# Attention, then routed experts, on one core: the causal mask of the transposed scores moves from TensorE to GpSimd, and the query and key products are laid over six steps

## The reference, cut to what matters

```
h = clip(curve(x @ ccm)) @ conv          # 8 pictures of 256 rows x 256, as tokens
h = concatenate([h, txt], axis=1)        # 8 x 384 tokens of 256 features
xn = layernorm(h)
ckv = xn @ W_DKV                         # 64 wide
q, k, v = xn @ W_UQ, ckv @ W_UK, ckv @ W_UV      # 16 heads of 16
scores = where(causal, q @ k.T / 4, -inf)        # per head, 384 x 384
h = h + (softmax(scores) @ v) @ W_O
h = h + moe(layernorm(h))                # 8 experts, top 2, capacity 384, gelu, 256-1024-256
```

## Time and profile before

| what | us |
|---|---|
| median of three runs | 706.63 |
| the profiled execution's own time | 704.81 |
| its span | 703.1 |
| TensorE busy in it | 639.8 (91%) |
| VectorE busy | 400.3 (57%) |
| ScalarE busy | 377.8 (54%) |
| GpSimd busy | 305.5 (43%) |

### The profile page before, as it was taken

The page is one execution under the profiler, slowest core; times in us unless marked ns, Lnnn a source line. Parts: engine busy times, 40 slices in busy tenths (PEclk is TensorE's granted clock), DMA queues, the critical chain, the costliest instruction groups (busy, mean ns, idle before and its releaser), DMA issues.

```text
span 703.1 us, 14382 instructions
## 1 busy us (share of the span) xinstructions
PE 639.8 (91%) x5488; PEld 533.9 (76%) x5488; DVE 400.3 (57%) x1005; ACT 377.8 (54%) x800; POOL 305.5 (43%) x415
## 2 busy tenths in 40 slices
PE   2799899998999999999988699999999999999991
PEld 2556565665666657567667699999999999999990
DVE  4887585687777877757766353444444444444310
ACT  4466766747667576565561265555555554555530
POOL 3300001004121141220426497888888888888222
PEclk9999999999999999999999889999999999999996
DMA  7448391714424043153103443444444444442222
GB/s 260 113 119 230 97 269 52 199 47 134 118 68 131 9 112 93 56 144 129 63 17 103 127 143 76 106 106 106 106 106 106 106 106 106 106 106 47 23 25 28
DMA packets 66477, 73.76 MB, mean 105 GB/s; under 512 B 6312, under 2 KB 61458, under 8 KB 66408
## 3 DMA queue, kind: packets, MB, share of 16 engines
q1 hardware_dynamic: 55584, 59.27, 27.8%
q0 software_dynamic: 9504, 13.00, 10.9%
q10 hardware_dynamic: 1320, 0.57, 0.3%
HBM read 31.62 MB, written 22.35 MB: 77 GB/s over the span
## 4 chain that ended last, share of the span: by engine, by line
PE 67%; DVE 12%; ACT 7%; issue 5%; DMA 3%; SPq 3%; POOL 1%; ACTq 0%; DVEq 0%; POOLq 0%
PE t_bank L1654 19%; PE bank L1669 12%; PE s_bank L1669 6%; PE bank L662 5%; DVE mx L1111 3%; PE t_bank L626 3%; PE t_bank L720 3%; SPq L392 3%; PE s_bank L604 3%; ACT part L978 2%; PE bank L690 2%; PE s_bank L1640 2%; DVE wr L1166 2%; PE t_bank L627 1%; PE s_bank L605 1%
## 5 line engine op out<-in xcount | busy, mean ns | idle before, releaser
L1613 DVE TENSOR_TENSOR hl<-h,hh 128x384 fp32r<-128x384 f32 x128 | 104.5, 818 | 155.7 <-ACT h L1571 155.7
L1111 DVE TENSOR_REDUCE mx<-s_bank 128x2 f32<-128x256 f32 (+2 forms) x192 | 122.6, 683 | 51.9 <-PE s_bank L605 51.3
L1568 ACT ACTIVATE hh<-t_bank 128x384 fp32r<-128x384 f32 x128 | 63.0, 492 | 133.9 <-PE t_bank L1654 131.7
L919 ACT ACTIVATE pt<-t_bank 128x512 f32<-128x512 f32 x128 | 76.8, 601 | 65.8 <-PE t_bank L627 64.8
L1538 POOL DMA_INDIRECT out<-yo,xr x48 | 75.0, 1564 | 72.6 <-ACT yo L1579 62.9
L1526 POOL TENSOR_TENSOR wl<-wr,wh 128x256 fp32r<-128x256 f32 x112 | 94.5, 878 | 1.2
L1654 PE MATMUL t_bank<-xh,wh 128*128 128x384 f32 x256 | 87.2, 341 | 0.0
L1654 PE MATMUL t_bank<-xl,wh 128*128 128x384 f32 x256 | 86.8, 339 | 0.0
L1654 PE MATMUL t_bank<-xh,wl 128*128 128x384 f32 x256 | 86.7, 338 | 0.0
L626 PE MATMUL t_bank<-qs,ks 98*128 98x384 bf16 (+2 forms) x384 | 85.2, 274 | 0.6 <-ACT pt L917 0.4
L604 PE MATMUL s_bank<-ks,qs 96*128 96x128 bf16 (+2 forms) x384 | 78.3, 273 | 5.4 <-DVE mx L1111 4.6
(11 more groups left out here) (191 smaller groups left out, 1433.6 us busy)
## 6 DMA issues: line engine op xcount, KB each, us to landing
wr<-in_w SPq DMA_DIRECT2D x16, 1024.0 KB, 5.7
qs<-part SPq DMA_DIRECT2D x96, 96.0 KB
ks<-part SPq DMA_DIRECT2D x90, 96.0 KB
slot_rows<-empty SPq DMA_DIRECT2D x4, 1560.0 KB, 9.3
xr<-slot_rows SPq DMA_DIRECT2D x16, 390.0 KB, 3.3
wr<-in_x SPq DMA_DIRECT2D x8, 768.0 KB, 5.4
out<-hid SPq DMA_DIRECT2D x8, 384.0 KB
qs<-mT ACTq DMA_DIRECT2D x64, 3.0 KB
```

Source lines behind the costliest of these rows:

```text
L919: ins = act.activation(pt[:, p, unit // 2, 0:AT[1]], bank, ACT.Exp)
L1111: ins = dve.tensor_reduce(mx[:, p // 2, j, 2 * (p % 2):2 * (p % 2) + 2], pair_region(s_bank, j), AX_X, ALU.max)
L1568: act.activation(hh[:, f, :], h_banks[f % NH], ACT.Gelu_apprx_tanh)
L1613: dve.tensor_tensor(hl[:, f, :], h[f % 2][:, :], hh[:, f, :].bitcast(F32), ALU.subtract).then_inc(hl_done, 1)
```

## The change

The mask matmul of line 627 and `mask_k` go. In their place GpSimd sets the part of each diagonal block that the mask hides to zero in `pt`, after the exponential, by an `affine_select` for each unit (`clip`: two blocks of 128 x 128, 192 calls in all), and `values` waits for those (`clipped`) and no longer for the exponentials. GpSimd's program is written anew around the clips: three in each step, with the sends, powers and bias additions between them, one bias addition behind each clip of p = 3.

The twelve stages of `query_key` stand two to a step (`ahead`): in the odd turn stage (0,0) at p = 1, then (0,1), (0,2) at p = 2, then (1,0), (1,1) at p = 3; in the even turn (1,2), (2,0) at p = 0, then (2,1), (2,2) at p = 1, then (3,0), (3,1) at p = 2, and (3,2) at p = 3. `project(b, 0)` goes to `M[1]`, both `token_values` and all `contexts_out` to `M[0]`, and `token_values(b + 1, 0)` moves from p = 1 of the even turn to its p = 0. The sync engine stacks k = 0 and 1 in the odd turn, and k = 2 and 3 in the even one.

```
+    def ahead(n, p, place):
+        b = n // 2 + (2 if n % 2 else 1)
+        i = 2 * p + place + (-3 if n % 2 else 5)
+        return (b, *divmod(i, 3)) if late(b) and 0 <= i < 12 else None
...
     def project_bank(b, k):
-        return s_bank[:, 2, :] if b == B - 1 and k else M[0]
+        if k == 0:
+            return M[1]
+        return s_bank[:, 2, :] if b == B - 1 else M[0]
...
                 elif live(b + 1):
-                    for i in range(3):
-                        stack(sp, b + 1, 3, i)
+                    for k in (2, 3):
+                        for i in range(3):
+                            stack(sp, b + 1, k, i)
...
+        def clip(n, p, unit):
+            pool.wait_ge(exp_done, 3 * (4 * n + p) + unit + 1)
+            if unit == 1:
+                blocks = pt[:, p, :, AT[1]:AT[1] + P]
+            else:
+                blocks = pt[:, p, unit // 2, 0:AT[1]].rearrange("p (i c) -> p i c", c=P)[:, 0:4:3, :]
+            pool.affine_select(out=blocks, in_=blocks, compare_op=ALU.is_ge, fill=0.0, base=0,
+                               pattern=[[0, 2], [1, P]], channel_multiplier=-1).then_inc(clipped, 1)
...
         for n in range(FIRST, LAST):
+            b, odd = n // 2, n % 2
+            for p in range(4):
+                for unit in range(3):
+                    if turn_live(n):
+                        clip(n, p, unit)
+                    if odd and (p, unit) == ((2, 0) if turn_live(n) else (0, 0)) and live(b - 1):
+                        rstds2(b - 1)
+                    if odd and p == 3 and live(b - 1) and b < B:
+                        residual(b - 1, unit)
+                if odd:
+                    if p == 1 and live(b - 2):
...
+                        send(b - 2, 0)
+                    if p == 2 and live(b - 2):
+                        send(b - 2, 1)
...
+                else:
+                    if p < 2 and live(b - 3) and n <= OVER:
+                        send(b - 3, 3 + p)
+                    if p == 2 and live(b + 2):
+                        rstds(b + 2)
+                    if p == 3 and live(b - 3) and n <= OVER:
+                        send(b - 3, 5)
...
     def shifted_scores(n, p, unit):
...
-                pe.matmul(bank[:, col:col + w], k[:, h, j * P:(j + 1) * P], q[:, h, j * P:T], start=True, stop=False)
-                mm = pe.matmul(bank[:, col:col + P], ident_b[:, :], mask_k[:, :], start=False, stop=True)
+                mm = pe.matmul(bank[:, col:col + w], k[:, h, j * P:(j + 1) * P], q[:, h, j * P:T], start=True, stop=True)
...
     def values(n, grp):
-            pe.wait_ge(exp_done, 3 * (4 * n + 2 * grp + 2))
+            pe.wait_ge(clipped, 3 * (4 * n + 2 * grp + 2))
```

More of the change, by code:

```diff
@@ L307, in front @@
     exp_done = sem("exp_done")
+    clipped = sem("clipped")
     pv_done = sem("pv_done")
@@ L456, in sync @@
                 elif live(b + 2):
-                    for k in range(3):
+                    for k in (0, 1):
                         for i in range(3):
@@ L549, in gpsimd @@
         for n in range(FIRST, LAST):
[L550 to L581, removed]
@@ new lines, in gpsimd @@
+            b, odd = n // 2, n % 2
[9 more added lines that the diff above has]
+                    if p == 1 and live(b - 2):
+                        if b == 2:
+                            pool.wait_ge(zeroed, 16 * (PIECES + 1))
+                        pool.wait_ge(slot_done, b - 1)
+                        send(b - 2, 0)
+                    if p == 2 and live(b - 2):
+                        send(b - 2, 1)
+                    if p == 3 and live(b - 2):
+                        if n < OVER:
+                            send(b - 2, 2)
+                        else:
+                            for i in range(2, TOPK * NT):
+                                send(b - 2, i)
+                else:
+                    if p < 2 and live(b - 3) and n <= OVER:
[4 more added lines that the diff above has]
+                        send(b - 3, 5)
@@ L685, in project @@
             pe.wait_ge(cn_sb, 2 * b + 2)
-            take("last" if b == B - 1 and k else 0, hid_add, 2 * b + k + 1)
+            take(1 if k == 0 else "last" if b == B - 1 else 0, hid_add, 2 * b + k + 1)
             dst = project_bank(b, k)
@@ L772, in tensor @@
         pe.wait_ge(consts, 5)
-        pe.wait_ge(masks, 6)
+        pe.wait_ge(masks, 4)
         pe.wait_ge(relu_done, CH)
@@ L816, in tensor @@
                     latents(b + 2, 1)
-                if odd and p >= 2 and late(b + 2):
-                    query_key(b + 2, p - 2, 2)
-                if not odd and p < 2 and late(b + 1):
-                    query_key(b + 1, 2 + p, 2)
+                if ahead(n, p, 0):
+                    query_key(*ahead(n, p, 0))
                 if n == FIRST and p == 3:
@@ L835, in tensor @@
                         query_key(1, k, 1)
-                if odd and late(b + 2):
-                    if p == 0:
-                        tokens_back(b + 2, 0, 1)
-                    else:
-                        query_key(b + 2, p - 1, 0)
-                if not odd and p == 0 and late(b + 1):
-                    query_key(b + 1, 3, 0)
+                if odd and p == 0 and late(b + 2):
+                    tokens_back(b + 2, 0, 1)
+                if ahead(n, p, 1):
+                    query_key(*ahead(n, p, 1))
                 if p == 0 and prev:
@@ L1021, in scalar @@
                 if p == 3 and prev:
-                    contexts_out(n - 1, 0 if odd else 1)
+                    contexts_out(n - 1, 0)
                 if odd and p == 1 and late(b + 2):
                     tokens_back(b + 2, 1, 1)
-                if odd and p >= 2 and late(b + 2):
-                    query_key(b + 2, p - 2, 1)
-                if not odd and p < 2 and late(b + 1):
-                    query_key(b + 1, 2 + p, 1)
                 if cur:
@@ L1055, in scalar @@
                     max_rows(n + 1, 0)
-                if odd and late(b + 2):
-                    if p == 0:
-                        tokens_back(b + 2, 0, 1)
-                    else:
-                        query_key(b + 2, p - 1, 0)
-                if not odd and p == 0 and late(b + 1):
-                    query_key(b + 1, 3, 0)
+                if odd and p == 0 and late(b + 2):
+                    tokens_back(b + 2, 0, 1)
+                if ahead(n, p, 1):
+                    query_key(*ahead(n, p, 1))
+                if not odd and p == 1 and live(b + 1):
+                    token_values(b + 1, 1, 0)
                 if n == 0 and p == 0:
@@ L1079, in scalar @@
                     contexts(n, 0)
+                if not odd and p == 0 and live(b + 1):
+                    token_values(b + 1, 0, 0)
                 if not odd and p == 0 and live(b + 2):
                     relus(b + 2, 0)
-                if not odd and p == 1 and live(b + 1):
-                    token_values(b + 1, 0, 0)
-                    token_values(b + 1, 1, 1)
                 if n == FIRST and p == 0:
```

31 lines of the change are left out of this document (9 added, 22 removed).

## The result

The changed kernel takes 693.01 us (median of four runs, 692.11 to 693.17), the one before 705.79 beside it (703.58 to 707.01): a ratio of 0.9826, with 95% between 0.9804 and 0.9849. The forecast was 686 us. The sign and the range held; the gain is 12.8 us where 21 were forecast. The profiled execution after took 693.07 us, 11.7 less than the 704.81 of before.

The account below looks back on a forecast made before the run. TensorE was taken to bound about 32 of each 44.6 us period, VectorE the other 12.6. Six periods gave 17 us and turns 0, 13, 14, 15 gave 4: 21 off 704.81, plus 1.8 to the median, 686 us; range 675 to 702.

Parts of the forecast that it names:

- The sum of the middle periods: Six two-turn periods with late batches: 3.3 us gained, less 0.3 port and 0.2 second norm, 2.8 each, 17 us in all.
- Spread and bank: Middle period: 0.4 us net from products moved out of TensorE's stretch, 0.8 from copy waits, 0.2 from the bank.
- the bank: Maxima's transpose waited 0.74 us for VectorE's row addition holding its bank; moving `project(b, 0)` was to save 0.2 a period.
- the 32 masks that matter: Of 48 mask matmuls a period, 32 lie where TensorE sets the pace: 0.058 us each, 1.86 us; the rest worth nothing.
- The 0.8 us for copies: TensorE's waits for ScalarE's copies of parts, 1.6 us a period, were to halve with two stages a step.
- Turns 0, 13, 14 and 15 have masks alone, 1.39 each, of which I count 1.0: 4.: Turns outside the six periods gain only from the removed masks, 4 us together.
- The values' matmuls show no wait for them: Sign: TensorE's value products never wait for clips, since 1.7 us separates exponential and values at p = 2, even turn.
- The colour steps: Sign: VectorE's colour steps, two inputs in SBUF, 736 to 794 ns in the turns, rise by at most a tenth.
- The port and the second norm: Losses a middle period: 0.3 us for VectorE's port shared with GpSimd, 0.2 for the norm's power queued behind a clip.
- Rival A: VectorE takes the period, so half the masks and none of the smoothing count: 8 us gained, 698; chance 0.17.
- Rival B: All 1.6 us of copy waits and 0.7 of the bank's go each period: 33 us gained, 673; chance 0.05.
- Rival C: GpSimd becomes late, TensorE waits for clips ahead of values: 14 us slower, 721; decides from 0.8 us clips; chance 0.10.

Follow-up runs that it names:

- experiment 10: The spread of the stages alone, both masks kept, with `project(b, 0)` back in `M[0]`; ratio 0.9923 to the kernel before.
- Experiment 4: The changed kernel with no clip run, diagonal blocks left unmasked and `values` waiting for the exponentials; 685.18 us, ratio 0.9718 to the kernel before.
- experiment 3: The changed kernel with odd-turn bias additions behind all clips of p = 3 on GpSimd and the first send a step later; 690.06 us, ratio 0.9791.
- experiment 1: The kernel before with only the clips in place of the second mask, stages and banks as they were; ratio 1.0006.
- experiment 6: The kernel before with one edit, the output projection of two tiles in the other bank; ratio 0.9940.
- experiment 2: The kernel before with only the spread of stages, new banks and stacking; both masks and the old GpSimd program stay; ratio 0.9844.
- experiment 8: The changed kernel with each clip done twice, the second after the first has ended; ratio 0.9997 to the kernel before.
- experiment 5: The changed kernel with odd-turn sends 0, 1, 2 and then the bias additions behind all clips of p = 3 on GpSimd; ratio 0.9798.

## Why the prediction was right in direction and 7 us off in size

**The sum of the middle periods held, its terms not quite.** 17 us were forecast, turns 1 to 12 gave 16.8; the period fell by 2.93 us, forecast 2.8. That it is so close is luck: two errors of 2 us cancel. Spread and bank brought 10.5 us where 6 x (0.4 + 0.8 + 0.2) = 8.4 were forecast. The term that was too small is the bank: I took 0.2 of a 0.74 us wait, and the wait of 0.80 us a period went entirely. How much of the 10.5 is the bank's is less sure, since experiment 10 has a delay of its own. The clips over the masks brought 6.3 on top where 6 x (1.86 - 0.3 - 0.2) = 8.2 were forecast. The price of the 32 masks that matter was too high, since part of their time came back as waits for copies. The 0.8 us for copies is right for the spread alone (1.48 to 0.72 a period) and wrong for the sum (1.38 with the masks gone): the masks that leave were part of the time in which the copies were made. Two terms that share a cover can't both be counted.

**The step that failed: "Turns 0, 13, 14 and 15 have masks alone, 1.39 each, of which I count 1.0: 4."** They lost 1.1 us. Experiment 4 splits it: without clips turn 0 is 0.3 and turns 13 to 15 are 1.9 us shorter than before, so the masks were worth 2.2 there, not 4. With clips the same parts are 0.8 and 2.4 us longer than without. The 2.4 us stand against a sum that had a price for clips only in six middle periods. The 0.8 us of turn 0 are not the clips' work: experiment 3 has the same clips there and takes 16.9 us against 16.8, and the profiled execution after has the 3.4 us at the lower clock. One execution of each kernel was profiled; such a fall in turn 0 stands in six of the ten kernels without the second mask (17.6 to 18.9 us; 16.2 to 17.0 in the other four) and in none of the four with it. That the emptier list lets it happen is likely, and not shown.

**What the sum did not have: the end of the turns.** Behind the last exponential 3.4 us were lost. "The values' matmuls show no wait for them" is right in the middle, where rows 4 and 7 had 1.7 us of cover, and wrong at the end: there the last value product is on the path, nothing runs beside it, and its clip stands behind a send and two bias additions. The wait for the clip (1.15 us) and the slow values (2.79 us for 1.50) are in the rows above. How much of the 3.4 us they are is less clear. 1.5 us come back in experiment 3 and 1.7 in experiment 4, without a clip; but experiment 1, with the wait and with values at full clock, takes 41.9 us, and so does experiment 6, without a clip. The other 1.7 or so is in experiments 2, 3 and 4 alike (40.4 to 40.6 against 38.7), with a granted clock of 0.71 in 370 to 380 us of experiment 2. The profiled execution of before stands at 0.50 for 8.0 us of this stretch, that of after for 14.8, and every other kernel profiled for 9.5 or more, with or without masks and clips. So a part of the 3.4 us can be that one execution's good fortune: four of the kernel before differ by 3.4 us (703.58 to 707.01). The prediction read no row of this stretch. The cause of the second half, and of the 1.0 us ahead of the first exponential (45.5 to 47.0 in all runs), stays open.

**Checked by the sum**: 21 forecast, less 0.2 (turns 1 to 12), 5.1 (bare turns), 3.4 (end), 1.0 (start), plus 0.3 (rest) is 11.6; measured 11.7. The profiled execution of before lies 1.0 us below the median of its four runs, that of after at its median, where I had allowed 1.8; so the profiled time missed 683.8 by 9.3 us, and the median missed 686 by 7.0.

**Smaller points.** A clip was forecast at 0.42 us; the median is 0.406. The colour steps' mean rose from 0.747 without clips to 0.791 us, 6%, under the tenth; but the long ones are mostly not the clips' doing, as the last section shows. The port and the second norm were 0.5 us a period; experiment 4, which takes away all of the clips' work, measures 0.3 for both together. The second norm alone waits 5.0 us for its power in eight waits, longest 2.0. The experts' part is unchanged. Rival A is out: VectorE waits 38.0 us for TensorE, and no part of the change shows it as the bound. Rival B overshoots by itself, but its idea that the bank's wait goes wholly was the right one. Rival C is shown by experiment 8 to exist at twice the price, mostly at the end of the turns, and with a smaller size.

## What to carry to other kernels

A pass taken off the bounding engine is worth only what no other wait on that engine was hiding behind it: measure it after the waits are cleared, as here, where the same masks were worth 0.26 us a middle period before and 1.09 after. Count a new step on a side engine in each phase of the pipeline, and above all where the pipeline drains: there its latency is on the path, and whatever stands in order in front of it too. Putting the work that the critical engine waits for first is worth trying in such a place, but look at what it delays. The runs here don't settle it: experiment 3 gained about 2.5 us by its ratio, at the edge of the noise and with the wait still there, and experiment 5 halved the wait and gained no more, since turn 14 became 3.7 us longer.

And look at the granted clock of each part before a difference is given to the change. Three of the losses here (turn 0, turn 14 of experiment 5, the stretch behind the turns) have time at 0.50 of full clock in them.

## What the runs showed of the hardware

A 12-column VectorE subtraction with both inputs in SBUF can take as long as GpSimd's instructions beside it. Before and after (ns min/median/max):

```profile
L1124 DVE TENSOR_TENSOR ms<-mx,ms x32: 148/150/221, 37.9 to 354.9; 128x12 bf16<-128x12 f32 x32
```

```profile
L1113 DVE TENSOR_TENSOR ms<-mx,ms x32: 147/151/1149, 39.0 to 339.5; 128x12 bf16<-128x12 f32 x32
```

One of the long ones, on VectorE, and what GpSimd ran beside it:

```profile
246.29 0.32 DVE L1113 TENSOR_TENSOR ms<-mx,ms 128x12 bf16<-128x12 f32 x1
```

```profile
245.85 0.72 POOL L520 TENSOR_TENSOR hid<-hid,prm 128x256 f32<-128x256 f32 x1
```

It ends at 246.61, as the addition does (246.57). All eight that took over 0.3 us started inside a GpSimd instruction. The Trainium skill (SBUF — State Buffer, "Who interferes with whom") calls the shared pair of ports an exclusive lock; the trace agrees. A small VectorE step that feeds TensorE, as this one does, is a bad place for it: TensorE's weight loads waited 0.3 us, once, for this step before, and 3.4 us in seven waits after.

The long steps of VectorE pay too, and more to the bias additions than to the clips. Of the 24 colour steps between 100 and 290 us of the changed kernel, five took 923 to 1003 ns, the others 753 or less; four of the five started inside a bias addition and one inside a clip. In experiment 2, without a clip, three took 1883 to 1922 ns, each beside two or three bias additions. So where GpSimd's other work falls counts for as much as the clips.
